# Normalised rows of a mixture-of-experts block kept in the channel order of the experts' weight runs

## The reference, cut to what matters

```python
xn = (x - mean) / sqrt(var + 1e-5)                    # per token
# attention part: random features, r = 0..511
feats = 1/sqrt(512) * exp(xis) * exp(xn @ (xis * proj).T - 0.5 * sum(xn * xn) * xis**2)
attn  = feats @ weights.T                             # weights: the same function of input_weights
# experts: router, best 4 of 8 groups, best 8 of 64 experts, at most 256 tokens each
scores = sigmoid(xn @ router_w)                       # top-k weights normalised, times 2.5
g, u   = dispatch[e] @ gate_w[e], dispatch[e] @ up_w[e]     # (256,512) @ (512,256)
routed = (silu(g) * u) @ down_w[e]                    # (256,256) @ (256,512), weighted, added to its tokens
shared = (silu(xn @ sgate_w) * (xn @ sup_w)) @ sdown_w
out = x + attn + routed + shared
```

## Time and profile before

| | |
|---|---|
| median of 3 runs | 1381.89 us (1376.86 to 1384.69) |
| profiled execution, its own time | 1375.42 us |
| its span, first to last instruction | 1373.7 us |
| mean granted TensorE clock | 0.992 |
| TensorE busy | 1337.6 us (97%) |
| VectorE busy | 860.4 us (63%) |
| ScalarE busy | 640.5 us (47%) |
| GpSimd busy | 503.5 us (37%) |
| moved by DMA | 250.00 MB |

### The profile page before, as it was taken

The page is one execution under the profiler, slowest core; times in us unless marked ns, Lnnn a source line. Parts: engine busy times, 40 slices in busy tenths (PEclk is TensorE's granted clock), DMA queues, the critical chain, the costliest instruction groups (busy, mean ns, idle before and its releaser), DMA issues.

```text
span 1373.7 us, 22484 instructions
## 1 busy us (share of the span) xinstructions
PE 1337.6 (97%) x7837; PEld 1168.8 (85%) x7837; DVE 860.4 (63%) x1661; ACT 640.5 (47%) x988; POOL 503.5 (37%) x347
## 2 busy tenths in 40 slices
PE   6899999999999999999999999999999999999995
PEld 4788888888888888888888999999999999999994
DVE  7765755666556665657535667766666666766662
ACT  5321222113221232212324677777777776777762
POOL 1200000000000000000002778767787787877763
PEclk9899999999999999999999999999999999999998
DMA  6361233213332233312224999999999999999995
GB/s 211 131 214 50 103 113 128 97 52 107 128 128 68 81 107 128 121 52 101 80 75 138 286 273 282 290 276 289 293 267 288 285 279 284 282 282 280 282 283 68
DMA packets 117501, 250.00 MB, mean 182 GB/s; under 512 B 31450, under 2 KB 34782, under 8 KB 117470
## 3 DMA queue, kind: packets, MB, share of 16 engines
q1 hardware_dynamic: 88798, 178.28, 38.3%
q0 software_dynamic: 28672, 71.32, 23.0%
HBM read 178.18 MB, written 71.39 MB: 182 GB/s over the span
## 4 chain that ended last, share of the span: by engine, by line
PE 93%; DVE 2%; SPq 2%; DMA 1%; issue 1%; ACT 1%; POOL 0%; POOLq 0%
PE pmm L1033 17%; PE pmm L1035 17%; PE pmm L1034 17%; PE pout L1033 11%; PE pout L1035 10%; PE pout L1034 10%; PE ptr L1248 4%; PE plog L1094 2%; PE ptr L1045 2%; SPq L338 1%; PE plog L1103 1%; DMA xbuf<-rows,slot_cols 1%; DMA outs<-n_L_ffn_shared_up_w_dram 0%; DMA out_dram<-outs,slot_cols 0%; POOL out_dram L1382 0%
## 5 line engine op out<-in xcount | busy, mean ns | idle before, releaser
L1382 POOL DMA_INDIRECT out_dram<-outs,slot_cols x128 | 269.3, 2104 | 122.7 <-DMA out_dram<-outs,slot_cols 92.9
L1033 PE MATMUL pmm<-xt_hi,proj_hi 128*128 128x256 f32 (+1 forms) x784 | 254.2, 324 | 4.3 <-DVE xt_lo L988 2.2
L1366 POOL TENSOR_TENSOR earlier<-earlier,chosen 128x64 bf16<-128x64 bf16 x64 | 28.6, 446 | 614.8 <-DVE chosen L758 611.0
L1033 PE MATMUL pmm<-xt_hi,sgu_hi 128*128 128x256 f32 (+1 forms) x768 | 251.8, 328 | 0.0
L1035 PE MATMUL pmm<-xt_hi,proj_lo 128*128 128x256 f32 (+1 forms) x784 | 250.8, 320 | 0.0
L1034 PE MATMUL pmm<-xt_lo,proj_hi 128*128 128x256 f32 (+1 forms) x784 | 250.8, 320 | 0.0
L1035 PE MATMUL pmm<-xt_hi,sgu_lo 128*128 128x256 f32 (+1 forms) x768 | 245.9, 320 | 0.0
L1034 PE MATMUL pmm<-xt_lo,sgu_hi 128*128 128x256 f32 (+1 forms) x768 | 245.3, 319 | 0.0
L1372 POOL DMA_INDIRECT xbuf<-rows,slot_cols x128 | 192.2, 1502 | 91.6 <-DVE slot_cols L801 38.6
L472 ACT ACTIVATE feat<-pmm,ab 128x512 f32<-128x512 f32 x68 | 46.9, 689 | 321.9 <-PE pmm L1035 317.8
L1033 PEld LDWEIGHTS pmm<-xt_hi,proj_hi 128*128 128x128 f32 x784 | 149.7, 191 | 16.1 <-DVE xt_lo L988 2.6
(11 more groups left out here) (180 smaller groups left out, 2559.6 us busy)
## 6 DMA issues: line engine op xcount, KB each, us to landing
raw<-in_L_ffn_gate_w_dram SPq DMA_DIRECT2D x64, 512.0 KB, 6.9
raw<-in_L_ffn_up_w_dram SPq DMA_DIRECT2D x64, 512.0 KB, 8.7
raw<-in_L_ffn_down_w_dram SPq DMA_DIRECT2D x64, 512.0 KB, 6.2
xbuf<-in_L_attn_x_dram SPq DMA_DIRECT2D x16, 1024.0 KB, 6.3
rows<-xn SPq DMA_DIRECT2D x16, 1024.0 KB, 4.2
outs<-in_L_attn_x_dram SPq DMA_DIRECT2D x32, 512.0 KB, 3.6
out_dram<-outs SPq DMA_DIRECT2D x32, 512.0 KB, 2.9
rows<-weight SPq DMA_DIRECT2D x16, 128.0 KB, 2.8
```

The costliest lines, as they stand in the source:

```text
L1033: pe.matmul(psum, lh, rh, start=first and n == 0, stop=False)
L1366: pool.tensor_tensor(after, earlier[b][:, j, :], chosen[:, j, :], ALU.add).then_inc(earlier_made, 1)
L1382: pool.indirect_dma_start(out=out, out_offset=bass.IndirectOffsetOnAxis(ap=slot_cols[:, at:at + 1], axis=0), in_=outs[e.b][:, c, :], in_of ...
```

## The change

The normalised row is written in another order. Columns 0 to 127 of `xn` hold channels 0, 4, 8 ... 508, column 128 the norm, and columns 129 to 512 the channels 1, 5 ..., then 2, 6 ..., then 3, 7 .... VectorE writes each block in two instructions that read `xbuf` at a stride of four words: one of 128 elements, one of 3 x 128. `turn_half` still reads columns 1 to 512, so the norm is now in half 0, and TensorE waits for `norm_made` ahead of half 0. The rows go to `rows` in two DMAs without the norm, and the experts' transposes read 128 contiguous columns. The projection is subtracted into the same order in eight instructions in place of two; the input weights are transposed with strided reads by a new `turn_iw`; router and shared weights are loaded with four consecutive rows per partition, the first shifted by four.

```diff
             def load_shifted(place, source, loaded):
-                full = (HB - 1) * P
-                sp.dma_start(place[:, 0:HB - 1], source[1:1 + full].rearrange("(c p) i -> p c i", p=P)).then_inc(
-                    loaded, 16)
-                sp.dma_start(place[0:P - 1, HB - 1], source[1 + full:]).then_inc(loaded, 16)
-                sp.dma_start(place[P - 1:P, HB - 1], source[0:1]).then_inc(loaded, 16)
+                rows4 = source.rearrange("(p c) i -> p c i", c=HB)
+                sp.dma_start(place[:, 1:HB], rows4[:, 1:HB]).then_inc(loaded, 16)
+                sp.dma_start(place[0:P - 1, 0], rows4[1:P, 0]).then_inc(loaded, 16)
+                sp.dma_start(place[P - 1:P, 0], source[0:1]).then_inc(loaded, 16)
...
             def store_xn(g):
                 sp.wait_ge(xn_made, g.n + 1)
-                sp.dma_start(rows_groups[g.n][:, :, 0:H], xn[:, :, 0:H]).then_inc(xn_stored, 16)
+                sp.dma_start(rows_groups[g.n][:, :, 0:P], xn[:, :, 0:P]).then_inc(xn_stored, 16)
+                sp.dma_start(rows_groups[g.n][:, :, P:H], xn[:, :, P + 1:]).then_inc(xn_stored, 16)
...
-                at_least(dve, xn_stored, 16 * g.n)
+                at_least(dve, xn_stored, 32 * g.n)
                 for j in range(J):
-                    ins = dve.tensor_scalar(xn[:, j, 0:H], xbuf[g.b][:, j, :], mean_var[:, j, 0:1],
-                                            rstd[:, j:j + 1], ALU.subtract, ALU.mult)
+                    row = xbuf[g.b][:, j, :].rearrange("p (q c) -> p c q", c=HB)
+                    for dst, source in ((xn[:, j, 0:P], row[:, 0]),
+                                        (xn[:, j, P + 1:].rearrange("p (c q) -> p c q", q=P), row[:, 1:])):
+                        ins = dve.tensor_scalar(dst, source, mean_var[:, j, 0:1], rstd[:, j:j + 1], ALU.subtract,
+                                                ALU.mult)
                 ins.then_inc(xn_made, 1)
                 step(dve.tensor_tensor(rstd2[:], rstd[:], rstd[:], ALU.mult), base)
-                dve.scalar_tensor_tensor(out=xn[:, :, H], in0=mean_var[:, :, 1], scalar=float(H),
+                dve.scalar_tensor_tensor(out=xn[:, :, P], in0=mean_var[:, :, 1], scalar=float(H),
...
-            less_first(xn[:, :, 1:H // 2 + 1], xbuf[1][:, :, 1:H // 2 + 1],
-                       xbuf[1][:, :, 0:1].to_broadcast([P, HB, H // 2])).then_inc(proj_copied, 1)
-            dve.wait_ge(proj_loaded[1], 16)
-            less_first(xn[:, :, H // 2 + 1:H], xbuf[1][:, :, H // 2 + 1:H],
-                       xbuf[1][:, :, 0:1].to_broadcast([P, HB, H // 2 - 1])).then_inc(proj_copied, 1)
+            for half in range(2):
+                dve.wait_ge(proj_loaded[half], 16)
+                for c in range(HB):
+                    at = (c * P + (c > 0)) + half * P // 2
+                    ins = less_first(xn[:, :, at:at + P // 2], xbuf[1][:, :, half * H // 2 + c:(half + 1) * H // 2:HB],
+                                     xbuf[1][:, :, 0:1].to_broadcast([P, J, P // 2]))
+                ins.then_inc(proj_copied, 1)
...
+            def turn_iw(half, psum, free):
+
+                at_least(pe, xt_lo_made, free)
+                for h in range(2):
+                    c = 2 * half + h
+                    for j in range(J):
+                        block = iw_raw[:, j, HB:H + 1:HB] if c == 0 else iw_raw[:, j, c:H:HB]
+                        ins = pe.transpose(psum[:, h, j * P:(j + 1) * P], block, ident[:])
+                ins.then_inc(turned, 1)
...
                 pe.wait_ge(xn_made, nxt.n + 1)
+                pe.wait_ge(norm_made, nxt.n + 1)
                 turn_half(nxt.n + 2, xn, 0)
...
                 shared_products(g, 0, 0)
-                pe.wait_ge(norm_made, nxt.n + 1)
                 turn_half(nxt.n + 2, xn, 1)
...
-            pe.wait_ge(proj_copied, 1)
+            pe.wait_ge(proj_copied, 2)
             turn_half(0, xn, 0, free=0)
-            pe.wait_ge(proj_copied, 2)
             turn_half(0, xn, 1, psum=pmm2, free=0)
...
-            pe.wait_ge(iw_loaded[0], 16)
-            turn_half(1, iw_raw, 0, psum=pout2, free=0)
-            pe.wait_ge(iw_loaded[1], 16)
             pe.wait_ge(pads_made, 1)
-            turn_half(1, iw_raw, 1, free=1)
+            for half in range(2):
+                pe.wait_ge(iw_loaded[half], 16)
+            turn_iw(0, pout2, 0)
+            turn_iw(1, ptr, 1)
...
-                        ins = pe.transpose(ptr_e[:, h, c * P:(c + 1) * P], xe[e.b][:, c, h:H:HB],
+                        ins = pe.transpose(ptr_e[:, h, c * P:(c + 1) * P], xe[e.b][:, c, h * P:(h + 1) * P],
```

More of the change, by code:

```diff
@@ L390, in _ @@
                 for half in range(2):
-                    at = slice(half * (H // 2 + 1), (H // 2 + 1, H)[half])
+                    at = slice(half * H // 2, (half + 1) * H // 2)
                     sp.dma_start(place[:, :, at], source.rearrange("(c p) d -> p c d", p=P)[:, :, at]).then_inc(
@@ L890, in _ @@
             step(dve.tensor_scalar(less[:, 0], ab[:], -0.5, None, ALU.mult))
-            dve.tensor_copy(xn[:, :, H], less[:, 0])
+            dve.tensor_copy(xn[:, :, P], less[:, 0])
             dve.wait_ge(ab2_exp, 1)
@@ L1222, in _ @@
                     pe.wait_ge(xn_made, 1)
+                    pe.wait_ge(norm_made, 1)
                     turn_half(2, xn, 0, psum=pout2, free=3)
-                    pe.wait_ge(norm_made, 1)
                     turn_half(2, xn, 1, free=4)
@@ L1387, in _ @@
             pool.wait_ge(slot_cols_made, 1)
-            pool.wait_ge(xn_stored, 16 * GROUPS)
+            pool.wait_ge(xn_stored, 32 * GROUPS)
             pool.wait_ge(w_stored, 16 * GROUPS)
```

## The result

The kernel became slower, by more than I forecast. The changed kernel has a median of 1446.63 us over four executions (1438.71 to 1467.92) against 1379.5 us for the kernel before (1376.86 to 1384.69): a ratio of 1.0453, interval 1.0385 to 1.0522. The forecast of 1414 us was 33 us low; its range, 1385 to 1448, held the time by 1.4 us.

A forecast was written before the change was run, and what follows sets the result against it. TensorE's queue was taken to bound both stages, other engines counting only where it waits. Groups 32.5 + first group 2.6 + start 0.9 - experts 4 = +32 us on the 1381.9 us median: 1414 us, range 1385 to 1448.

The forecast's parts named there:

- Direction and place: Dense stage: slower, as TensorE waits for VectorE at each group's first transposes; 2.3 us x 14 groups = 32.5 us.
- The experts, -4: Expert stage: contiguous transposes gain 5.1 us at most, of which 4 us was kept because gathers might land late.
- Fixed cost of an instruction, 0.195 us: VectorE's normalisation: each instruction costs 0.195 us fixed, so eight cost 1.56 us per group where it was 0.78.
- Rate, slow for 3 x 128 and fast for 128: VectorE's normalisation: 1.07 ns per element for the 3x128 pieces, 0.51 ns for the 128s, before any stride cost.
- Stride, +0.53 ns per element and half of it at the fast rate: VectorE's reads of every fourth word: extra cost per element, taken from TensorE's weight load; group total +2.6 us.
- From norm to weight load, 0.05 us: Dense stage: TensorE's weight load starts 0.05 us after what it waits for, part of a 2.5 us stall.
- The start, 3.5 us: Start and first group: +2.6 us ahead of the router's choice and +0.9 us left from subtraction and first normalisation.
- At nothing: Second row store, scratch rows, and shared and router loads in rows of three: 0, the loads within 1 us.
- The clock case: Rival: dense stalls also halve TensorE's clock, +24 us, or stride costs its upper bound, +22; 1426 to 1460 us, chance 0.18.
- Only one of rate and stride: Rival: in VectorE's normalisation just the slow rate or just the stride costs, +17 or +12 us; 1394 to 1399, chance 0.20.
- hides: Rival: VectorE's normalisation, at fast rate and free stride, mostly hides; +4 us, 1386, or 1378 if instructions are free; chance 0.17.
- late gathers end last: Rival: in the expert stage the gain is lost to gathers; +4 us on any case, inside their ranges, no own chance.

The follow-up runs named there:

- e10: Changed kernel with VectorE's order changed: next group's deviations before the first low half of the features, normalisation before the second; median 1387.89 us, ratio 1.0064.
- e6: Kernel before, with five extra statistics instructions on VectorE ahead of the normalisation, into an unread tile; 1486.64 and 1436.93 us.
- e3: Changed kernel with the experts' transposes reading every fourth column again, as before; ratio 1.0483.
- e4: Changed kernel, normalisation still in eight instructions but reading contiguous columns; four executions took 1387.81 to 1440.42 us.
- e5: Changed kernel with one normalising instruction of four strided runs of 128 per block in place of two; 1421.7 and 1448.26 us.
- e9: Kernel before, with only the wait for the norm moved ahead of the first transposes; 1376.36 and 1376.52 us, ratio 0.9984.
- e1: The changed kernel run once more, unaltered, against the kernel before; its profiled execution took 1438.68 us, ratio 1.0434.
- e7: Kernel before, with three extra statistics instructions on VectorE ahead of the normalisation, into an unread tile; 1393.74 and 1393.61 us, ratio 1.0118.
- e12: Kernel before, ScalarE copying finished rows into the experts' order, first copy behind the first group's features, experts reading contiguously; median 1372.46 us, ratio 0.9952.
- e8: Kernel before, ScalarE copying finished rows into the experts' order, first copy ahead of rounding the shared weights, experts reading contiguously; median 1393.38 us, ratio 1.0104.

## Why the prediction was right or wrong

- **Direction and place: right.** TensorE's wait for VectorE at the first transposes of each group is the loss. e10 takes the lateness away and keeps all the work: 43.67 us. e6 puts the lateness in and has none of the change: 47.7 us.
- **The experts, -4: right.** 3.3 us shorter than before, 3.8 us shorter than e3. The experts' weight load is at 141 ns, as forecast. That GpSimd's gathers would take some of it back was not seen in the profiled executions compared here.
- **Fixed cost of an instruction, 0.195 us: right.** In e4 (347 ns for 128 and 480 ns for 384 contiguous elements) an element costs (480 - 347) / 256 = 0.52 ns, the fast rate of 0.51, and a group's eight instructions take 2.58 us until the next one starts (459.01 to 461.59): (2.58 - 2048 x 0.52 ns) / 8 = 0.19 us each.
- **Rate, slow for 3 x 128 and fast for 128: right** by e4 and e5. With 3 strided runs of 128 it is 956 ns, with 4 only 737. The Trainium skill, "VectorE: DVE Perf Modes", section "What auto-detection actually checks", has this even-or-equal rule; the runs agree with it, with those two numbers.
- **Stride, +0.53 ns per element and half of it at the fast rate: too small.** The eight instructions take 4.67 us until the next one starts (489.15 to 493.82), where the sum had 4.42, and 1.82 before. A row of a single instruction overlaps the next by some 0.09 us (544 ns long, 0.455 apart); 956 less 0.09 is 0.87 us for a 3 x 128, and (0.87 - 0.195) / 384 = 1.75 ns per element, so 0.68 on top of 1.07. The price was taken from TensorE's weight load, and was the nearest row but not the right one: +2.85 and not +2.6. The Trainium skill, "Vector Engine (DVE) Microarchitecture Reference", section "Measured stream behaviour on trn2", gives 1.73 ns, measured there on an operation with two sources; the 1.75 of this trace agrees. The +2.9 that I worked out from that figure comes to 2.8 by my own sum (1.56 + 0.40 + 1536 x 1.73 ns - 1.82), and the trace has 2.85.
- **From norm to weight load, 0.05 us: too small.** It is 0.22 to 0.23 (e9 and the rows above). The 0.05 came from a place where TensorE waited for xt_lo. With the two corrections the stall is 2.85 + 0.03 + 0.22 - 0.17 = 2.9 by my own step; 2.74 was measured. The forecast was 2.5.
- **The step that failed: the clock was left out of the sum.** I had seen it in the earlier trace rows, with a price of 1.7 us, and gave it a chance of 0.18 because the stall was "shorter than that one" (3.04). The trace of before has another stall, of 2.20 us at the start of the experts, which I left out, with no stretch at half clock behind it (none lies between 64.5 and 1361 us):

```profile
744.08 0.39 PE L1033 MATMUL pmm<-xt_hi,proj_hi 128*128 128x256 f32 x1 [2.20 <-DVE xt_lo L988]
```

  So the stall of 2.5 us lay between one of 2.20 without and one of 3.04 with, and nothing of before said which it would follow: that calls for a chance near one half and not 0.18. In e1 the same wait as at 744 us (2.28 us, at 810.38) has a stretch behind it. In the groups it happened behind 13 of the 14 stalls, and in e6, with 2.46 us each, behind all but one. From the first transposes of a group to the second it now takes 5.31 us (446.28 to 451.59) or 5.19, and before 3.78 with a wait of 0.43 inside: +1.4 to +1.5 where I had -0.19. With the stall, 2.74 + 1.47 = 4.2 us in each of 14 groups, 59 us; the forecast was 2.3 x 14 = 32.5. The 1.47 are again two terms: the clock costs 1.57 by the two kinds of group in e6, and the stall returns 0.10 by e7, where the clock was left alone (508.79 to 512.47 is 3.68 us where it was 3.78). My 1.7 was half of 3.41 us; the count beside it, ten products in place of some fifteen, is 1.2 us at 0.235 each, and the two do not agree. The measured 1.57 lies between them.
- **The start, 3.5 us: half of it.** It is 7.4 (e10). The eight subtractions with two sources took 4.18 us where two took 2.44, close to the 1.5 that I had added. What I had put at nothing behind them was not nothing: the first transposes of the projection wait for both halves now, their first weight load comes at 9.3 us and not at 6.8, and the first normalisation starts at 26.14 us where it was 23.34. So VectorE reaches the preparation of the shared weights at 32.41 us and not at 30.07, 2.3 later and not 0.9. The rest is in the first group, where TensorE waits 5.44 us for the rows; it has two stretches at half clock there (at 57.3 and 67.5 us, in e10 too) and had one; on the other hand the one of 6.83 us from 33.78 us on in the trace of before is gone. How much each of these gives to the 7.4 was not taken apart:

```profile
5.03 4.18 DVE L668 TENSOR_TENSOR xn<-xbuf 128x256 f32<-128x256 f32 x8
57.43 1.94 PE L1050 MATMUL ptr<-ident,xn 128*128 128x128 f32 x8 [5.44 <-DVE xn L721]
```

- **At nothing: the second store of each group, the loads' new runs, the scratch rows: right,** since e10 has them all and its groups are as long as before. That speaks for the groups; what the loads do at the start lies inside the 7.4.
- **The rivals.** The clock case, 1426 to 1460 us, came true with its mechanism and about its size: I had +24 if all groups pay, and 14 x 1.57 = 22 of the 59 - 32.5 = 26.5 us that the groups cost beyond the forecast are that; the rest is mostly the longer stall. The range held the time because it had been drawn over most of this case, not because the sum was near: the sum has +32 where the medians are 67.1 us apart. "Only one of rate and stride" is out by e4 and e5, "hides" by everything. That late gathers end last is seen in single executions of the changed kernel (22.5 us of waits above) and of most versions, and whether the change makes it more frequent is open.

The account of the difference of the two spans: 7.4 for the start, 59.0 for the groups, -3.3 for the experts, together 63.1 of 63.3 us.

## What to carry to other kernels

Where an engine already hands over its result just in time, work added to it has two prices: the wait, and, behind waits of 2.2 us and more here, mostly a slow stretch of TensorE too; look in the trace of before for all stalls of about that length, see what followed each, and put the second price into the sum with the chance that they give it. A layout that a reader would like is best made by the engine with room (ScalarE here, in e12), or by the same engine early enough (e10, in the groups), and not by the one on which TensorE waits. And ask of each strided operation which rate it runs at: with four strided runs an element cost 0.89 ns and with three 1.75, 0.33 us for 384 of them, more than the 0.195 us of a whole instruction.

## What the runs showed of the hardware that I had not expected

- A stall of TensorE of 2.4 to 3.1 us was followed by a stretch of 3.41 us or more at half clock in 13 of 14 groups, one of 1.28 us never was in the groups of e7; between e7 and e6 1.2 us of VectorE's work cost 2.8 us per group. Near 2.2 to 2.4 us the same wait goes either way: with no stretch behind it at 744.08 us in before (2.20) and at 110.32 us in e1 (2.43), with one behind it at 810.38 (2.28) and 733.33 us (2.41) in e1.
- VectorE's reads of every fourth word cost a factor of 1.6 to 1.7 at either rate (1.75 against 1.07 ns in the 3 x 128s, 0.51 + 0.38 = 0.89 against 0.51 in e5), while every second word was free in an operation with two sources. Every fourth word costs there too: the subtractions of the start in e1, with two sources and every fourth word, are 0.51 us apart for 256 elements, (0.51 - 0.075) / 256 = 1.7 ns each. ScalarE has it too: 3917 ns for 2048 elements at a stride of four in e8, against 1910 ns for a contiguous copy of 2048 (L567 in before).
- Single executions of the same kernel were up to 55 us apart (1377.38 to 1432.38 for the kernel before on one chip); in the changed kernel's long execution TensorE is less busy in the expert stage (89.47 of 100 us). That is ten times what the change could win there.
